# The first unit's queries and keys by feature groups, and its first stacks loaded ahead of storing the other heads' parts

## The reference, cut to what matters

```
h      = layernorm(x) * (1 + scale) + shift          # scale, shift, gate: silu(c) @ wmod
q,k,v  = h @ Wq, h @ Wk, h @ Wv                      # 16 heads of 16
s      = (q k^T + alibi) / 4, causal; w = softmax(s) # layer 0; layer 1 has rotary q,k instead of alibi
x      = x + gate * (w v) @ Wo
h2     = layernorm(x) * (1 + scale2) + shift2
layer 0: x = x + gate2 * sigmoid(xr Wr) * (relu(xk Wk)^2 Wv)   # xr, xk: mixes of h2 and its shift by a token
layer 1: x = x + gate2 * (h2 @ (W + low-rank product) + b)
```

## Time and profile before

| what | us |
|---|---|
| median of 3 runs | 2794.85 |
| the profiled execution | 2790.14 |
| its span | 2788.4 |
| TensorE busy | 2464.7 |
| VectorE busy | 2156.4 |
| ScalarE busy | 1711.5 |
| GpSimd busy | 1025.8 |

### The profile page before, as it was taken

One profiled execution on the slowest core, in us unless ns is written; L12 is line 12 of the kernel. 1 busy time (PEld: TensorE's weight loads), 2 busy tenths in 40 slices (PEclk: granted clock), 3 DMA queues, 4 the chain that ended last, 5 costly groups with the idle time before them and its releaser, 6 DMA issues.

```text
span 2788.4 us, 55137 instructions
## 1 busy us (share of the span) xinstructions
PE 2464.7 (88%) x18968; PEld 1027.6 (37%) x18968; DVE 2156.4 (77%) x6588; ACT 1711.5 (61%) x3458; POOL 1025.8 (37%) x1558
## 2 busy tenths in 40 slices
PE   6898888988999999988999989999999989897686
PEld 4323333423334343343434333443433434333223
DVE  3897758788887988878887988878888788872961
ACT  3475575555765667756675666656677566664264
POOL 4222542244242443335243442434433352335222
PEclk9999999999999999999999999999999999998788
DMA  6510143121413222311423214131223114004000
GB/s 213 171 58 20 37 130 99 34 80 48 139 48 101 62 89 83 111 49 50 122 67 93 77 53 139 54 104 51 88 83 111 49 50 136 21 29 136 30 2 16
DMA packets 142394, 218.29 MB, mean 78 GB/s; under 512 B 21190, under 2 KB 62556, under 8 KB 142052
## 3 DMA queue, kind: packets, MB, share of 16 engines
q1 hardware_dynamic: 142120, 214.77, 25.5%
HBM read 137.87 MB, written 77.89 MB: 77 GB/s over the span
## 4 chain that ended last, share of the span: by engine, by line
PE 54%; DVE 24%; ACT 10%; issue 5%; POOL 5%; DMA 1%; SPq 0%; DVEq 0%; POOLq 0%; ACTq 0%
PE ctx_ps L1649 11%; PE big L1630 11%; PE big L1567 10%; DVE small L1398 8%; PE big L1556 8%; PE small L1608 7%; ACT probs L1184 6%; DVE mx L1396 4%; PE big L1681 4%; ACT xn L1233 4%; DVE stats L1352 3%; PE big L1664 2%; DVE region L1461 2%; DVE mx L1398 1%; DVE region L1499 1%
## 5 line engine op out<-in xcount | busy, mean ns | idle before, releaser
L1184 ACT ACTIVATE probs<-big 128x512 f32<-128x512 f32 (+2 forms) x2560 | 1221.4, 563 | 429.9 <-PE big L1630 421.4
L1398 DVE CUSTOM_DVE_ANT_0 small<-small,mask 128x128 f32<-128x128 f32 (+3 forms) x2048 | 942.9, 520 | 141.6 <-PE small L1608 130.7
L1630 PE MATMUL big<-stack_q,stack_k 64*128 64x512 f16 (+3 forms) x6144 | 711.8, 330 | 81.1 <-ACT probs L1184 52.8
L1396 DVE TENSOR_REDUCE mx<-small 128x1 f32<-128x512 f32 x1024 | 652.1, 682 | 102.8 <-PE small L1608 96.5
L1649 PE MATMUL ctx_ps<-probs,v_ones 128*17 128x512 f32 (+3 forms) x6144 | 646.6, 498 | 28.8 <-POOL probs L1063 19.3
L1063 POOL TENSOR_SCALAR_AFFINE_SELECT probs<-probs 128x512 f32<-128x512 f32 x512 | 329.0, 653 | 674.4 <-ACT probs L1184 674.1
L1608 PE MATMUL small<-stack_k,stack_q 64*128 64x512 f16 (+3 forms) x3072 | 458.0, 335 | 130.9 <-DVE mx L1398 76.0
L1630 PEld LDWEIGHTS big<-stack_q,stack_k 64*128 64x128 f16 x6144 | 232.0, 95 | 610.5 <-issue 356.5
L1608 PEld LDWEIGHTS small<-stack_k,stack_q 64*128 64x128 f16 x3072 | 128.9, 94 | 549.6 <-DVE mx L1398 248.7
L1398 DVE DVE_READ_ACCUMULATOR2_ANT mx<- 128x1 f32 x2048 | 286.2, 140 | 0.0
L1556 PE MATMUL big<-hT,w_qkv 128*128 128x512 f32 x512 | 274.3, 640 | 1.5 <-ACT probs L1184 1.4
(11 more groups left out here) (94 smaller groups left out, 1938.6 us busy)
## 6 DMA issues: line engine op xcount, KB each, us to landing
image<-region SPq DMA_DIRECT2D x192, 256.0 KB
stack_q<-image SPq DMA_DIRECT2D x64, 512.0 KB, 3.8
stack_k<-image SPq DMA_DIRECT2D x64, 512.0 KB, 4.7
lo_dram<-region SPq DMA_DIRECT2D x64, 256.0 KB
w_qkv<-wqkv SPq DMA_DIRECT2D x16, 768.0 KB, 6.4
x_res<-x SPq DMA_DIRECT2D x32, 256.0 KB, 3.5
stack_q<-lo_dram SPq DMA_DIRECT2D x128, 64.0 KB, 4.2
stack_k<-lo_dram SPq DMA_DIRECT2D x128, 64.0 KB, 5.2
```

The source lines that it names most:

```text
L1184: s.activation(probs[:, n % HELD, heads, q0:], big[:, at.slot(turn), 0:len(pairs) * width] .rearrange("p (h q) -> p h q", h=len(pairs)), A ...
L1396: last = v.reduce_max(to, held, AX)
L1398: last = v.tensor_tensor_reduce(out=held, in0=held, in1=mask[:, BANK - width:], scale=1.0, scalar=3.0 * NEG, op0=ALU.add, op1=ALU.max, acc ...
L1630: last = te.matmul(big[:, at.slot(at.turn() + parity), j * width:(j + 1) * width], stack_k[rows, c, g * PAIR_N + pair, kt * P:(kt + 1) * P ...
```

## The change

For unit 0 alone there is a new sequence, `first_sequence`. The layer norm statistics and chains of both halves come first, then the transposes of block 0, then xn of the second half. Queries and keys go by feature group: for ft = 0 both token blocks of queries and keys, then their stores; then ft = 1, the values, and the stores of ft = 1. Stacks 0 and 1 hold the heads of ft = 0; they wait for their own stores alone (a new semaphore `early_saved`), and the second group's stores may be planned only behind the load of stack 1. Max items of any unit are planned only behind the last value of unit 0. `spill`, the post loads of unit 0, the layer 1 constant rows and x of batch 2 are issued behind `pre_loads` of unit 1. The modulation of layer 0 is cut in two: the part for the first layer norm in `mods`, the rest with the gates in once 0; wmod of layer 0 gets another place in SBUF. GpSimd's clearing of stack_k becomes four memsets.

```diff
+def first_sequence():
+    first, second = layernorm_items(0, 0, 0, NT // 2), layernorm_items(0, 0, NT // 2, NT)
+    out = first + second[:-NT // 2] + turned(0, 0, 0) + second[-NT // 2:]
+    for ft in range(FC):
+        for tb in range(2):
+            out += turned(0, 0, 1) if (ft, tb) == (0, 1) else []
+            out += [(kind, 0, w, ft, tb) for w in range(2) for kind in ("qk", "hi", "split")]
+        out += [("value", 0, half, n) for half in range(2) for n in range(2)] if ft else []
+        out += [("parts_save", 0, w, ft) for w in range(2)]
+    return out + [("pre_loads", 1)]
+def save_of(unit, g):
+    return [("parts_save", unit, w, *((g // 2,) if unit == 0 else ())) for w in range(2)]
+def saved_early(item):
+    return item[0] == "parts_save" and item[3:] == (0,)
...
# Model.other
+            if item[1] == 1:
+                self.ready["post_loads", 0] = self.moved(self.run("SP", begin, 2600), 2400, 0.180)
...
# barred
+        if kind == "parts_save" and item[2:] == (0, 1):
+            return ("stack_load", 0, 1) not in seen
...
# follow: stack loads
+                saved = model.at(*save_of(u, g))
+                if save_of(u, g)[1] not in seen or (u and ("last", u - 1, g) not in seen) \
+                        or (u, g // 2) != (0, 0) and saved > max(now, model.free["SP"]) + EASE:
...
-                if ("stack", *item[1:3]) not in model.ready:
+                if ("stack", *item[1:3]) not in model.ready or ("value", 0, 1, 1) not in seen:
...
# with_start
-    out += [("x_load", 1, n) for n in range(4)] + [("once_in", 0)] + [("x_load", 2, n) for n in range(4)]
+    out += [("x_load", 1, n) for n in range(4)] + [("once_in", 0)]
-    after = {("stack_load", 0, 0): [("spill", 0), ("post_loads", 0)]}
+    after = {("pre_loads", 1): [("spill", 0), ("post_loads", 0), ("fixed_rows", 1)] + [("x_load", 2, n) for n in range(4)]}
...
# SyncE, stack_load
+                    if not unit:
+                        sp.wait_ge(early_saved, 16 * SAVE_DMAS)
+                    if unit or g >= NG // 2:
+                        sp.wait_ge(parts_saved, at.now("parts_save", 0, 16 * SAVE_DMAS))
...
# GpSimd
-            g.memset(stack_k[:, 1], 0.0).then_inc(stacks_clear, 1)
+            for g_ in range(NG):
+                g.memset(stack_k[:, 1, g_ * PAIR_N:(g_ + 1) * PAIR_N], 0.0).then_inc(stacks_clear, 1)
...
# TensorE
             def once(n):
                 if n == 0:
+                    modulations(0, (1, 3))
+                    gates_of(0, ctx_ps[0:B])
...
                 if kind == "mods":
-                    modulations(0).then_inc(mods_mm, 1)
-                    gates_of(0, ctx_ps[0:B])
+                    modulations(0, (0, 2)).then_inc(mods_mm, 1)
```

More of the change, by code:

```diff
@@ L272, in other_needs @@
         if kind == "parts_save":
-            return max(self.at(("split", *item[1:], ft, tb)) for ft in range(FC) for tb in range(2)), "SP"
+            return max(self.at(("split", *item[1:3], ft, tb)) for ft in item[3:] or range(FC) for tb in range(2)), "SP"
         if kind == "ln":
@@ L330, in other @@
             self.ready[kind, item[1]] = self.moved(self.run("SP", begin, 450), 768, 0.180)
+            if item[1] == 1:
+                self.ready["post_loads", 0] = self.moved(self.run("SP", begin, 2600), 2400, 0.180)
         elif kind == "parts_save":
-            self.ready[kind, item[1], item[2]] = self.moved(self.run("SP", begin, 3600), 2048, 0.180)
+            self.ready[item] = self.moved(self.run("SP", begin, 3600), 1024 if item[3:] else 2048, 0.180)
     def bank(self, end):
@@ L450, in barred @@
         if kind in ("scale", "bias"):
-            return (("post_loads", unit) if unit else ("stack_load", 0, 0)) not in seen or open_("pre", unit, "ln")
+            return (("post_loads", unit) if unit else ("pre_loads", 1)) not in seen or open_("pre", unit, "ln")
         return False
@@ L543, in plan @@
                       if n in ("pre", "post") and q and not on_pe(q[0]) and not barred(n, q[0])]
-            times += [model.at(("parts_save", l[0], 0), ("parts_save", l[0], 1)) for l in loads[:1] if ("parts_save", l[0], 1) in seen]
+            times += [model.at(*save_of(*l)) for l in loads[:1] if save_of(*l)[1] in seen]
             assert times, ({k: q[:2] for k, q in queues.items()}, to_join[:2], to_turn, later, loads[:2])
@@ L631, in events @@
         e["turn"] = 2 if kind == "score" else 1
+    if kind == "parts_save" and item[3:]:
+        del e[kind]
+        if item[2]:
+            e["early_save" if saved_early(item) else kind] = 1
     if kind == "max":
@@ L836, in adaln_program @@
         parts_saved = sem("parts_saved")
+        early_saved = sem("early_saved")
         stacked = [sem(f"stacked_{g}") for g in range(NG)]
@@ L927, in step @@
                 elif kind == "fixed_rows":
-                    sp.wait_ge(stacks_clear, 2)
                     for w in range(2):
-                        for l in range(LAYERS):
-                            sp.dma_start(image[w, l, :, ROW_ALIBI:], tail_rows[w * (1 + l)])\
-                                .then_inc(rows_in, 16)
+                        sp.dma_start(image[w, item[1], :, ROW_ALIBI:], tail_rows[w * (1 + item[1])]).then_inc(rows_in, 16)
+                    if item[1]:
+                        return
+                    sp.wait_ge(stacks_clear, 1 + NG)
                     for parity in range(2):
@@ L977, in step @@
                     own = qk_place(layer, w)[1]
-                    for ft in range(FC):
+                    saved = early_saved if saved_early(item) else parts_saved
+                    for ft in item[3:] or range(FC):
                         heads, half = slice(ft * HH, (ft + 1) * HH), slice(0, DH)
@@ L984, in step @@
                             sp.dma_start(image[w, layer, heads, n * DH + half.start:n * DH + half.stop], own[:, ft, s])\
-                                .then_inc(parts_saved, 16)
-                        sp.dma_start(lo_dram[w, layer, heads, half], own[:, ft, 1]).then_inc(parts_saved, 16)
+                                .then_inc(saved, 16)
+                        sp.dma_start(lo_dram[w, layer, heads, half], own[:, ft, 1]).then_inc(saved, 16)
                 elif kind == "stack_load":
@@ L1221, in step @@
                         if unit or layer and w:
-                            act.wait_ge(parts_saved, (2 * unit + layer * w) * 16 * SAVE_DMAS)
+                            act.wait_ge(early_saved, 16 * SAVE_DMAS)
+                            act.wait_ge(parts_saved, (2 * unit + layer * w - 1) * 16 * SAVE_DMAS)
                         if at.own("y_add"):
@@ L1375, in modulate @@
                     wait_all_emptied(dve, at, [at.turns[i] for i in turned(unit - 1, which)])
-                cols = modT[:, 8 * layer:8 * layer + 8, batch:batch + 1]
-                v.tensor_copy(modc[:, which], cols.rearrange("p k o -> p (k o)")).then_inc(modc_ready, 1)
+                cols = modT[:, 8 * layer:8 * layer + 8, batch:batch + 1].rearrange("p (h w c) o -> p h w (c o)", h=2, w=2)
+                own = modc[:, which].rearrange("p (h w c) -> p h w c", h=2, w=2)
+                v.tensor_copy(own[:, :, which], cols[:, :, which]).then_inc(modc_ready, 1)
             def step(at, item):
@@ L1508, in _, with modulations @@
             pe.wait_ge(consts_set, 3)
-            def modulations(l):
-                for k, part in enumerate((0, 3, 1, 4)):
+            def modulations(l, which):
+                for k in which:
+                    part = (0, 3, 1, 4)[k]
                     for fc in range(FC):
```

36 lines of the change are left out of this document (19 added, 17 removed).

## The result

The kernel after takes 2814.26 us (median of 4 runs, 2809.53 to 2817.18); the kernel before, on the same chip, 2793.61 (2789.76 to 2794.88). The ratio is 1.0075, with a 95% interval of 1.0055 to 1.0095: slower by 20.6 us, where I had forecast 2790.0 and a range up to 2802. The profiled execution took 2817.18 us with a span of 2815.3.

A forecast was written before the change was run, and what follows sets the result against it. PE was taken as nearest to the bound, though not full, with DVE close. The middle of DVE's 8.2 us and PE's 1.3 us gain, 4.8 us, off the 2794.85 median gave 2790.0 us; range 2780 to 2802.

The forecast's parts named there:

- Steps 1 to 3: Start-up: layer norm, queries and keys ending at 39.7, moved matmuls costing 3.8 us; last value at 63.7, gaining 1.3 us.
- the clock falls earlier: Rival, chance 0.18: in the once blocks PE's clock is at 0.50 from the moved matmuls, costing 9.0 us; 2802.5.
- Step 4: First stores from 34.7, landed 47.9; stack 0 there by 58.9; first max at 63.7 on PE, 14.4 us earlier.
- Step 5: SyncE's later queue: stack 2 landed at 114.7, needed at 118; w_qkv costs up to 8 us, taken as 0.
- Step 6: Unit 1's layer norm behind two max items on DVE: transposes at 80 instead of 72, PE idle 13.7 us.
- a sign that the gain nears 14: Unit 1's layer norm still running in front of the first max would prove the forecast wrong, with gain near 14 us.
- The sum: Whole kernel: 8.2 us gained seen from DVE, 1.3 seen from PE; the middle, 4.8 us, was taken.
- The term I had at 4 us: PE idle from 65 to 111: what DVE's pace costs once unit 1's projections run, at least 0, taken as 4.
- equal stretches: Behind 111 us PE and DVE are equally full; stretches behind 200 differing in length would prove the forecast wrong.
- The left-over case: Behind the start: the planner's order changes everywhere, with either sign; chance 0.02, put to slower, no size given.

The follow-up runs named there:

- e10: Kernel after, with only the planner's belief on the first unit's row maxima set to the fixed delays of e8; 2807.59 us.
- e8: Kernel after, w_qkv of unit 1 issued before the second group's stores, planner's beliefs changed on w_qkv, first stack loads and unit 0's row maxima (fixed delays); 2790.64 us.
- e11: e9 with only the planner's four delays for the first unit's row maxima set to what e9's trace showed; 2775.05 us.
- e1: Kernel after, with only the planner's belief on w_qkv of unit 1 changed, to 19.5 us after unit 0's last value instead of 34; 2803.88 us.
- e12: Kernel before, with only the planner's belief on the second head group's row maxima made 20 us later; 2814.09 us.
- e9: e8 with unit 1's layer norm listed in front of the first unit's values; 2799.33 us.

## Why the prediction was wrong

*Steps 1 to 3, the start: right, with too little gain.* Queries and keys ended at 40.5 (forecast 39.7), the last value at 60.8 (forecast 63.7). The difference is the clock. By 2 us in after, the columns of the earlier trace rows:

```profile
50.00:52.00 2.00, 2.00 (x18) 1.94 (x18) 0.09 (x1) 0.00 (x0) 0.00 (x0) 1.00 0.05 17
52.00:54.00 2.00, 2.00 (x9) 1.58 (x8) 1.89 (x8) 0.00 (x0) 0.00 (x0) 0.56 0.96 319
54.00:56.00 2.00, 2.00 (x12) 1.88 (x10) 1.97 (x4) 0.00 (x0) 0.00 (x0) 0.59 1.00 278
56.00:58.00 2.00, 2.00 (x13) 1.61 (x14) 1.97 (x3) 0.60 (x1) 0.00 (x0) 1.00 1.04 281
```

It was low for 4 us and then 1.00 again, so the last 32 value matmuls took 3.84 instead of 5.36. The rival "the clock falls earlier" was wrong at its place: the moved thin matmuls ran at 1.00 (1.85 for sixteen at 40.29).

*Step 4, stores and loads: right.* Stores from 36.14 (34.7), the load of stack 0 issued at 50.77 (47.9). Stacks 0 and 1 had landed by 62.31, when SP's wait for them ended. The early load did what it says.

*Step 5, SP: right in its doubt, wrong in what I took from it.* I had given w_qkv 8 us at full length and took 0. It was issued at 72.54 because the second group's stores first wait for the stacks to land (a wait of `parts_save` that I didn't list), and they took 10 us to issue. PE was not hurt by this on the chip, since it didn't want w_qkv before 104.

*Step 6, the layer norm: the gap was right, the reason not.* I had forecast PE idle between the last value and the transposes, because two max items and the layer norm would stand in a row on DVE. The gap was there (10.44 us) and the first max came at 74.87, not at 64. But the statistics of unit 1 didn't wait for max items; they ran at 58.14, behind the gates' work on DVE. The list had put transposes in front of the first max, so the max items waited for xn. The gain at the first max was 3.2 us instead of 14.4. I had named a layer norm in front of the first max as a sign that the gain nears 14; it came true, and the gain didn't follow.

*The sum: here it failed.* In it I took it that unit 1's projections run once the transposes are done, at 80, and that DVE's pace then costs PE "at least 0; I take 4". That took their place in the list from the kernel before. But the list is made anew, from the planner's beliefs, and I had read its code for the layer norm and not for w_qkv. On the planner's own clock (not a chip time) w_qkv of unit 1 arrives 34 us after the last value in after and 14 us in before, since the loads of stacks 0 and 1 and eight stores now stand ahead of it on the one queue that it models. So 20 max items and the first rows came before the first projection. The term I had at 4 us is, as idle time of PE from 78 to 111, 33 - 17.26 = 15.7, and the matmuls that did run took longer: 0.61 for a max item instead of 0.39. (From 65 to 111 PE idles 8.2 + 15.7 = 23.9 us; before had 15.4, and the sum had 13.7 + 4 = 17.7. Besides, PE did other work than the sum had: max items alone, with the projections left for later.) Behind 111 I had assumed equal stretches; PE idles 11.7 us there against 8.1, and the belief on the first score's rows costs some of it (e10).

*The left-over case.* "The planner's order changes everywhere behind the start, with either sign" got 0.02, without a size. It was the case that happened. In a kernel whose list is written by a planner it deserved its own rival, its place (`moved`, the single queue) and a price, for which the earlier trace rows had the pieces: DVE at 32.04 of 33.00 with PE at 24.77, and in the trace of before 16.98 us of these 24.77 are matmuls with w_qkv, which PE has to make up later if they are taken out.

*What was right about the mechanism.* With the beliefs mended the change and an earlier w_qkv come to 2790.64 (e8), which is no change against before: the early load costs nothing then, and a gain of it isn't shown. With the layer norm that step 6 named as next late, moved up as well, the time is 2775.05 (e11), but by 200 us that is worth only some 4 us; the other 14 come from the plan behind it and would be luck to claim for the mechanism. That 2790.64 is also nearly the 2790.0 forecast is luck too: the forecast was for another kernel, with projections at their old place.

## What to carry to other kernels

Where a planner orders the instructions, a change of transfers acts twice: on the chip, and through what the planner believes of them. Read from the code when it will believe each moved transfer to be there, and compare in the trace the time at which an operand landed with the time at which it was first used: the 23 and 39 us between them here led to most of the loss (some 17 of 20.6 us, by e1 and e10, if the two add up). And when the bound engine of a phase (DVE with max items) has a partner with other work to do, the price of a wrong order is the partner's idle time, plus what it loses in clock. And where a plan is made anew with each edit, test a cause at the stretch where it acts: the total of a run also holds what the new plan does elsewhere, here up to 14 us.

## What the runs showed of the hardware

PE's granted clock stayed at 0.50 (1.2 GHz) through the stretch in which it had only max items. In before it was 1.00 (2.4 GHz) there: DVE was as full, but projections stood between the max items. Stretch 78 to 104, after first, then before:

```profile
78.00:104.00 26.00, 11.15 (x49) 2.15 (x49) 24.60 (x77) 0.00 (x0) 0.00 (x0) 0.50 0.81 251
```

```profile
78.00:104.00 26.00, 19.83 (x78) 5.61 (x77) 25.07 (x84) 8.36 (x14) 14.81 (x13) 1.00 0.83 236
```

In after the clock had not fallen there. It was at 0.50 already at 66 to 70, when PE stood idle, and max items alone didn't bring it back. The fall itself is seen in e12, where PE came from 1.00 and no pause between max items was longer than 1.76 us. First after, then three stretches of e12:

```profile
66.00:70.00 4.00, 0.00 (x0) 0.00 (x0) 0.00 (x0) 2.83 (x6) 0.84 (x4) 0.50 0.66 182
```

```profile
148.00:150.00 2.00, 0.24 (x6) 0.11 (x4) 1.97 (x6) 0.00 (x0) 0.64 (x1) 1.00 0.71 224
150.00:152.00 2.00, 0.84 (x8) 0.13 (x4) 2.00 (x11) 0.00 (x0) 0.00 (x0) 0.58 0.04 14
152.00:154.00 2.00, 0.61 (x2) 0.10 (x2) 2.00 (x9) 0.00 (x0) 0.00 (x0) 0.50 0.02 4
```

By the Trainium skill, page "TensorE: Matmul & The Clock Gate", section "What's actually happening", the throttled state is the default and activity releases it; the two rows of 78 to 104 agree. They say nothing on the fall at 52 to 56, where PE was busy all the time.

A small transfer can be late through its queue alone: in e9 the first rows were written at 96.67, and SyncE sent them at 110.84. For 4.7 us of that it stood in a wait of stores ahead in its list, and for 9.4 us it issued them: eight stores of 256 KB, each three of which held it for 2 to 5 us.
